# A level-embedding, attention and ternary-FFN tower on one core: load order, ScalarE's DMA queue, output copies and the written order of five engines changed

## The chip, the cores and the metric

One core of a Trainium2 chip runs the whole program once per launch. The metric is the device time of one execution in microseconds (us). Three runs of the kernel before gave 53.23, 53.73 and 56.08 us; their median, 53.73 us, is what the change is measured against.

## The reference, cut to what matters

Sixteen sequences of 128 token ids go in, a float32 array of shape [16, 128, 256] comes out.

```
level[b, s] = running count of open minus close brackets, clipped to 0..31        # a scan over s
h  = 0.15 * level_emb[level]                                                       # a table of 32 rows x 256
h  = h + attention(layernorm(h))      # 16 query heads of 16, 4 key/value heads; Wq, Wk, Wv, Wo, biases
W1t, W2t = ternary(W1), ternary(W2)   # clip(round(W / (mean|W| + eps)), -1, 1)
h  = h + relu(layernorm(h) @ W1t.T + b1) @ W2t.T + b2                              # 256 -> 1024 -> 256
```

A row of h depends on its level and its sequence alone, so everything is computed per sequence and level (16 x 32 = 512 rows), and the last step copies each row to the tokens that have its level.

## The kernel before, in words

The 16 sequences are taken as four groups g of four (NG = 4, BG = 4); a group has 128 rows, four sequences of 32 levels. The feed-forward part (FFN) works on two halves of 256 rows, hidden features in eight chunks of 128. No loop is left to a scheduler: each engine has a list of calls written out by hand (from line 457 for GpSimd, 598 for ScalarE, 956 for VectorE, 1300 for TensorE, 345 for SyncE), runs it strictly in that order, and meets the others at semaphores only. A call that waits holds up all that stands behind it on its engine.

The stages, with the names that the steps use:

- **Loads.** SyncE issues the table, Wq, Wk, Wv, bv, bk, then W1 in two halves, W2 in two halves, Wo, the broadcast table and biases (lines 345 to 362). ScalarE's queue issues the tokens (one load that reads x three times, into 48 partitions) and bq. Each load has a semaphore.
- **Levels.** `open_tokens`, `token_drops`, `drops`, `level_scan`, `level_ends`, `end_codes`, `gone_levels`, `level_onehot`, `count_blocks`, `counts`, `counts_out`: the scan, its smallest and largest level, a one-hot matrix and the number of tokens at each level.
- **Table and scores.** `table_stats` to `norm_table` normalise 32 table rows, `table_t` transposes them, `keys` and `queries` project them. `key_blocks` (line 793) adds bk and waits for its load. `key_hi`, `key_lo`, `query_lo` split into high and low parts. `scores`, `scores_t(g)`, `prefix_max`, `prefix_t`, `prefix_out`, `maxima`, `max_hi`, `max_parts`, `less_max` give each score less its maximum.
- **Attention.** `exps(g)`, `counted_values(g)` on GpSimd, `context(g)`, `inverse_sums(g)`, `normalise(g)`, `context_t(g)`, `ctx_out(g)`, `out_proj(g)`, `add_table(g)`, then the second layer norm: `row_stats`, `row_moments`, `variance_eps`, `inverse_root` (GpSimd), `norm_rows`, `rows_t`, `x_hi`, `x_lo`.
- **Ternary weights.** `magnitudes(w, i)` sums |W| of one half (ScalarE, waits for that half's load), `abs_total(w)` adds over partitions, `threshold(w)` makes the threshold and, for W1, the inverse. W1 is rounded by ScalarE (`rounded(q)`, then `ternary(q)`), W2 by VectorE (`signs(i)`, then `ternary(0..3)`). `weights_t(u)` transposes an eighth of the two matrices on TensorE, `weights_out(u)` copies it out.
- **FFN.** `ffn1(h, j)` is four matmuls of half h and chunk j; `hidden(h, j)` applies relu and b1, `hidden_lo(h, j)` splits; `ffn2(j, g)` adds two matmuls into the accumulator of group g. `final(g)` adds the residual.
- **Output.** `spread(g)` multiplies one-hot and final rows, four matmuls to four PSUM banks. `result(g)`: ScalarE copies sequences 0 and 1 to SBUF, VectorE 2 and 3. Each pair of sequences is one store of 256 KB, eight in all, the first of group 3 on ScalarE's queue (`last_store`), the others on SyncE's.

TensorE also runs matmuls of zeros (`warm_up`, `keep_warm`) where it would stand idle early on.

Of the kernel before, what the change touches and what calls it, by code (L numbers as in the profile page):

```python
# [27 lines left out]
P = 128  # L28
# [8 lines left out]
def level_tower(nc, x, emb, Wq, bq, Wk, bk, Wv, bv, Wo, bo, W1, b1, W2, b2, out):  # L37
# [20 lines left out]
    with ctx:  # L58
# [285 lines left out]
        def _(sp):  # L344
            sp.dma_start(emb1[:], emb).then_inc(d_emb, 16)
            sp.dma_start(wq[:], Wq.rearrange("(c p) n -> p c n", p=P)).then_inc(d_wq, 16)
            sp.dma_start(wk1[:], Wk.rearrange("(c p) n -> p c n", p=P)).then_inc(d_wk, 16)
            sp.dma_start(wv[:], Wv.rearrange("(c p) n -> p c n", p=P)).then_inc(d_wv, 16)
            sp.dma_start(bvr[:], bv.unsqueeze(0)).then_inc(d_bv, 16)
            sp.dma_start(bkc[:], bk.unsqueeze(0).unsqueeze(2).to_broadcast([2, KVD, 1])).then_inc(d_bk, 16)  # L350
            for i in range(2):
                c = slice(i * FC // 2, (i + 1) * FC // 2)
                sp.dma_start(w1[:, c, :], w1_rows[:, c, :]).then_inc(d_w1[i], 16)
            for i in range(2):
                sp.dma_start(w2[:, i, :], w2_rows[:, i, :]).then_inc(d_w2[i], 16)
# [9 lines left out]
            for g in range(NG):  # L365
                b0 = g * BG
# [8 lines left out]
        def _(pool):  # L375
# [80 lines left out]

            sequence_index()
            rounding_terms()
            level_index()
            diagonal_index()  # L460
            partition_index()
            column_index()
            ones_f32()
            level_replicas()
            root_power()
            table_root()
            ones_bf16()
            clip_bounds()
            scan_resets()
            group_selectors()  # L470
            table_copies()
            counted_values(0)
# [15 lines left out]
        def _(act):  # L488
            act.dma_start(tok3[:], x.unsqueeze(0).to_broadcast([3, B, S])).then_inc(d_tok, 16)
            act.dma_start(bq2[:], bq.rearrange("(k a e d) -> a e k d", k=KV, a=2, e=2)).then_inc(d_bq, 16)  # L490

# [61 lines left out]
            def last_store():  # L553
                b0 = (NG - 1) * BG
                act.wait_ge(a_out, NG)
# [42 lines left out]
            key_weights()  # L598
            query_weights(0)
            rows_out()  # L600
            query_weights(1)
            table_load()
# [3 lines left out]
            prefix_out()  # L606
            magnitudes(0, 1)
            max_hi()
            magnitudes(1, 0)
            magnitudes(1, 1)  # L610
            exps(0)
            exps(1)
            exps(2)
            rounded(0)
            ctx_out(0)
            ctx_out(1)
            exps(3)
            rounded(1)
            ternary(0)
            ctx_out(2)  # L620
            ternary(1)
            weights_out(0)
            ctx_out(3)
            x_hi(0)
            weights_out(1)
            x_hi(1)
            weights_out(2)
# [6 lines left out]
            hidden(0, 3)  # L634
            hidden(0, 4)
            norm_rows(2)
            hidden(0, 5)
            norm_rows(3)
            weights_out(6)
            x_hi(2)  # L640
            x_hi(3)
            hidden(0, 6)
# [4 lines left out]
            hidden(1, 2)  # L647
            hidden(1, 3)
            hidden(1, 4)
            final_hi(0)  # L650
            hidden(1, 5)
            hidden(1, 6)
            result(0)
            final_hi(1)
# [7 lines left out]
        def _(dve):  # L662
# [71 lines left out]
            def open_tokens():  # L734
                dve.wait_ge(d_tok, 16)
# [213 lines left out]
            def result(g):  # L949
                for b in range(2, BG):  # L950
                    dve.wait_ge(p_out, g * BG + b + 1)
                    ins = V.tensor_copy(osb[:, g, b, :], out_banks(g)[b][:, 0:D])  # L952
# [473 lines left out]
```

## Time and profile before

| what | value |
|---|---|
| median of 3 runs | 53.73 us (53.23 to 56.08) |
| profiled execution, its own time | 54.04 us |
| its span, first to last instruction | 52.0 us |
| TensorE busy | 45.6 us (88%), 394 matmuls |
| VectorE busy | 38.0 us (73%) |
| ScalarE busy | 34.2 us (66%) |
| GpSimd busy | 15.7 us (30%) |
| bytes moved | 5.37 MB, 103 GB/s over the span |
| share of TensorE in the chain that ended last | 76% |

The span is what the trace shows of one execution; 2.04 us of the execution's time lie around it. Busy shares are averages over stages with different limits. A busy TensorE is not one at its peak, and the matmuls of zeros count as busy. The chain of waits is followed back from the last instruction: each piece was released by the one before it.

### The profile page before, as it was taken

Reading aid. Unit: us, or ns where it says so; the run is one execution under the profiler, and the core shown is the slowest. Engines: PE = TensorE matmul, PEld = TensorE weight load, DVE = VectorE, ACT = ScalarE, POOL = GpSimd, SP = SyncE. Lnnn points to the kernel's source line nnn. Section 1 sums busy time; section 2 is a strip of 40 time slices with the busy share of each in tenths; the row PEclk is TensorE's granted clock in tenths of the full one; section 3 lists DMA queues with packets and bytes.
Section 4 is the critical chain, followed back from the end, with each engine's and each line's share of the span. In section 5 each row is a group of like instructions: output and inputs, shape, how many; then the busy total and the mean of one; then the engine's idle time right before and its main releaser. Section 6 shows DMA issues by size and latency. Waiting matters only on the chain.

```text
span 52.0 us, 1206 instructions
## 1 busy us (share of the span) xinstructions
PE 45.6 (88%) x394; PEld 36.3 (70%) x394; DVE 38.0 (73%) x141; ACT 34.2 (66%) x77; POOL 15.7 (30%) x37
## 2 busy tenths in 40 slices
PE   0999999999999799999999999999999999993000
PEld 0336469894758688768679999989999798860000
DVE  3558994698985289999999996269858889659100
ACT  0083231380799997989988999999967793509000
POOL 5689952000005950009200579970000000000000
PEclk9999999999999999999999999999999999999997
DMA  0183919999753100000000000000000005555893
GB/s 0 36 234 77 44 63 350 410 432 368 198 124 98 47 7 0 0 0 0 0 0 13 0 0 0 0 6 0 0 0 0 0 13 200 203 208 195 295 385 127
DMA packets 4658, 5.37 MB, mean 103 GB/s; under 512 B 1117, under 2 KB 4141, under 8 KB 4653
## 3 DMA queue, kind: packets, MB, share of 16 engines
q1 hardware_dynamic: 4312, 5.02, 31.2%
q10 hardware_dynamic: 341, 0.29, 1.6%
q8 instruction: 3, 0.05, 0.4%
q14 instruction: 2, 0.02, 0.1%
HBM read 3.21 MB, written 2.10 MB: 102 GB/s over the span
## 4 chain that ended last, share of the span: by engine, by line
PE 76%; DVE 10%; POOL 3%; issue 1%; ACT 1%; DVEq 1%
PE pswt L1258 16%; PE psmisc L1273 15%; PE psg L1067 8%; PE psg L1063 5%; PE psg L1194 4%; POOL rs L445 3%; PE psg L1240 3%; DVE aw L952 2%; PE psg L1106 2%; PE psg L1153 2%; PE psg L1203 2%; PE psg L1154 2%; PE psg L1158 2%; DVE cn L892 2%; DVE hq L906 2%; DVE st L910 2%
## 5 line engine op out<-in xcount | busy, mean ns | idle before, releaser
L587 ACT ACTIVATE hr<-pswt,b1c 128x256 f32<-128x256 f32 x16 | 7.6, 484 | 1.2 <-PE pswt L1258 0.9
L1273 PE MATMUL psmisc<-w2T,hh 128*128 128x256 f32 x32 | 8.2, 285 | 0.0
L1273 PE MATMUL psmisc<-w2T,hl 128*128 128x256 f32 x32 | 8.1, 281 | 0.0
L937 DVE TENSOR_TENSOR hl<-hr,hh 128x256 fp32r<-128x256 f32 x16 | 6.7, 435 | 1.2 <-ACT hh L589 0.9
L1258 PE MATMUL pswt<-xhi,w1T 128*128 128x256 f32 x32 | 7.0, 299 | 0.0
L1258 PE MATMUL pswt<-xlo,w1T 128*128 128x256 f32 x32 | 6.4, 280 | 0.0
L1273 PEld LDWEIGHTS psmisc<-w2T,hh 128*128 128x128 f32 x32 | 6.0, 189 | 0.1
L1273 PEld LDWEIGHTS psmisc<-w2T,hl 128*128 128x128 f32 x32 | 6.0, 189 | 0.0
L445 POOL TENSOR_TENSOR rs<-ve,mhalf 128x1 f32<-128x1 f32 x4 | 2.7, 686 | 9.1 <-DVE ve L918 9.1
L440 POOL TENSOR_TENSOR voc<-vo,cpos 128x272 f32<-128x272 f32 x4 | 2.7, 714 | 8.1 <-DVE cpos L858 8.1
L1258 PEld LDWEIGHTS pswt<-xhi,w1T 128*128 128x128 f32 x32 | 4.9, 189 | 0.3
L1258 PEld LDWEIGHTS pswt<-xlo,w1T 128*128 128x128 f32 x32 | 4.9, 188 | 0.0
L1067 PE MATMUL psg<-warm 128*128 128x256 bf16 x24 | 4.7, 352 | 0.0
L528 ACT ACTIVATE aw<-w 128x1024 f32<-128x1024 f32 x4 | 4.2, 1055 | 0.0
L1194 PE MATMUL psg<-wo,cT 128*128 128x256 f32 x16 | 4.2, 394 | 0.0
L594 ACT ACTIVATE aw<-psg 128x256 f32<-128x256 f32 x6 | 2.0, 381 | 2.9 <-PE psg L1298 1.6
L1067 PEld LDWEIGHTS psg<-warm 128*128 128x128 bf16 x24 | 2.8, 126 | 1.5 <-issue 0.8
L1063 PE MATMUL psg<-warm 128*128 128x512 bf16 x6 | 2.7, 630 | 1.2 <-DVE tiny L666 1.2
L589 ACT ACTIVATE hh<-pswt,b1c 128x256 fp32r<-128x256 f32 x7 | 3.4, 482 | 0.0
L502 ACT ACT_TABLE_LOAD x1 | 1.3, 1283 | 2.8 <-issue 2.8
L1194 PEld LDWEIGHTS psg<-wo,cT 128*128 128x128 f32 x16 | 2.8, 190 | 0.3
L455 POOL TENSOR_TENSOR hb<-hq,b_bc 128x256 f32<-128x256 f32 x4 | 3.0, 782 | 0.0
(177 smaller groups left out, 108.4 us busy)
## 6 DMA issues: line engine op xcount, KB each, us to landing
w<-in_L_ffn_W_dram SPq DMA_DIRECT2D x4, 512.0 KB, 6.8
out_dram<-aw SPq DMA_DIRECT2D x7, 256.0 KB, 2.4
wq<-in_L_attn_Wq_dram SPq DMA_DIRECT2D x1, 256.0 KB, 3.5
wo<-in_L_attn_Wo_dram SPq DMA_DIRECT2D x4, 64.0 KB
out_dram<-aw ACTq DMA_DIRECT2D x1, 256.0 KB, 2.9
emb<-in_L_tok_level_emb_dram SPq DMA_DIRECT2D x1, 128.0 KB
bo_bc<-in_L_attn_bo_dram SPq DMA_DIRECT2D x1, 128.0 KB, 8.8
b_bc<-in_L_ffn_b_dram SPq DMA_DIRECT2D x1, 128.0 KB, 7.3
```

The costliest lines, as they stand in the source:

```text
L440: nc.gpsimd.tensor_tensor(voc[:, bs, :], vo[:].unsqueeze(1).to_broadcast([P, BG, VW]), cpos[:, bs].unsqueeze(2).to_broadcast([P, BG, VW]), ...
L445: nc.gpsimd.tensor_tensor(rs2[:, g:g + 1], ve2[:, g:g + 1], mhalf[:], ALU.pow).then_inc(g_rs2, 1)
L455: nc.gpsimd.tensor_tensor(hb[:, g, :], hq[:, g, :], b2_bc[:], ALU.add).then_inc(g_hb, 1)
L528: nc.scalar.activation(aw[:, w, i * 1024:(i + 1) * 1024], halves(w, i), ACT.Abs, accum_out=asum[:, 2 * w + i:2 * w + i + 1]).then_inc(a_ab ...
L587: nc.scalar.activation(hr[:, n % NHR, :], pswt[n % 2][:, 0:RH], ACT.Relu, bias=b1c[:, j:j + 1]).then_inc(a_hr, 1)
L589: nc.scalar.activation(hh[:, n, :], pswt[n % 2][:, 0:RH], ACT.Relu, bias=b1c[:, j:j + 1]).then_inc(a_hh, 1)
L937: V.tensor_tensor(hl[:, n, :], hr[:, n % NHR, :], hh[:, n, :].bitcast(F32), ALU.subtract).then_inc(v_hl, 1)
L1063: mm(bank[:, :], warm[:, 0:P], warm[:], start=True, stop=True)
L1067: mm(bank[:, 0:256], warm[:, 0:P], warm[:, 0:256], start=True, stop=True)
L1194: ins = mm(psg[g][:, 0:D], cT[:, g, e].rearrange("p b l -> p (b l)"), wo[:, e, :], start=(e == 0), stop=(e == H2 - 1))
L1258: ins = mm(pswt[n % 2][:, 0:RH], w1T[:, j, k, :], part[:, k, HALF * h:HALF * (h + 1), :].rearrange("p g n -> p (g n)"), start=(m == 0 and ...
L1273: ins = mm(psmisc[r][:, 0:D], part[:, n, r * P:(r + 1) * P], w2T[:, j, :], start=(j == 0 and m == 0), stop=(j == FC - 1 and m == 1))
```

## The change

The computation is the same. Four things differ.

- **Loads.** SyncE issues table, Wq, W1 (two), bv, W2 (two), and the rest as before. Wk, Wv and bk go to ScalarE's queue, and the tokens are three loads of 16 partitions in place of one.
- **Copies.** `result(g)` has ScalarE copy sequences 0 and 2, VectorE 1 and 3, with a semaphore step at each copy.
- **Stores.** A pair's store waits for one copy of each engine; the waits of `spread` and `last_store` follow.
- **Written orders.** All four compute engines get new lists.

```diff
@@ sync
             sp.dma_start(emb1[:], emb).then_inc(d_emb, 16)
             sp.dma_start(wq[:], Wq.rearrange("(c p) n -> p c n", p=P)).then_inc(d_wq, 16)
-            sp.dma_start(wk1[:], Wk.rearrange("(c p) n -> p c n", p=P)).then_inc(d_wk, 16)
-            sp.dma_start(wv[:], Wv.rearrange("(c p) n -> p c n", p=P)).then_inc(d_wv, 16)
-            sp.dma_start(bvr[:], bv.unsqueeze(0)).then_inc(d_bv, 16)
-            sp.dma_start(bkc[:], bk.unsqueeze(0).unsqueeze(2).to_broadcast([2, KVD, 1])).then_inc(d_bk, 16)
             for i in range(2):
                 c = slice(i * FC // 2, (i + 1) * FC // 2)
                 sp.dma_start(w1[:, c, :], w1_rows[:, c, :]).then_inc(d_w1[i], 16)
+            sp.dma_start(bvr[:], bv.unsqueeze(0)).then_inc(d_bv, 16)
             for i in range(2):
                 sp.dma_start(w2[:, i, :], w2_rows[:, i, :]).then_inc(d_w2[i], 16)
...
-                if g < NG - 1:
-                    sp.wait_ge(a_out, g + 1)
-                    sp.dma_start(out_t[:, b0:b0 + 2, :], osb[:, g, 0:2, :]).then_inc(d_out, 16)
-                sp.wait_ge(v_out, g + 1)
-                sp.dma_start(out_t[:, b0 + 2:b0 + 4, :], osb[:, g, 2:4, :]).then_inc(d_out, 16)
+                for e in range(2):
+                    if g == NG - 1 and e == 0:
+                        continue
+                    b0 = g * BG + 2 * e
+                    sp.wait_ge(a_out, 2 * g + e + 1)
+                    sp.wait_ge(v_out, 2 * g + e + 1)
+                    sp.dma_start(out_t[:, b0:b0 + 2, :], osb[:, g, 2 * e:2 * e + 2, :]).then_inc(d_out, 16)
@@ scalar
-            act.dma_start(tok3[:], x.unsqueeze(0).to_broadcast([3, B, S])).then_inc(d_tok, 16)
+            for i in range(3):
+                act.dma_start(tok3[B * i:B * i + B, :], x).then_inc(d_tok, 16)
+            act.dma_start(wk1[:], Wk.rearrange("(c p) n -> p c n", p=P)).then_inc(d_wk, 16)
+            act.dma_start(wv[:], Wv.rearrange("(c p) n -> p c n", p=P)).then_inc(d_wv, 16)
             act.dma_start(bq2[:], bq.rearrange("(k a e d) -> a e k d", k=KV, a=2, e=2)).then_inc(d_bq, 16)
+            act.dma_start(bkc[:], bk.unsqueeze(0).unsqueeze(2).to_broadcast([2, KVD, 1])).then_inc(d_bk, 16)
...
-                act.wait_ge(a_out, NG)
+                act.wait_ge(a_out, 2 * NG - 1)
+                act.wait_ge(v_out, 2 * NG - 1)
...
-                for b in range(2):
+                for b in range(0, BG, 2):
                     act.wait_ge(p_out, g * BG + b + 1)
-                    ins = nc.scalar.activation(osb[:, g, b, :], out_banks(g)[b][:, 0:D], ACT.Copy)
-                ins.then_inc(a_out, 1)
+                    nc.scalar.activation(osb[:, g, b, :], out_banks(g)[b][:, 0:D], ACT.Copy).then_inc(a_out, 1)
@@ vector: open_tokens waits for 48 in place of 16; result(g)
-                for b in range(2, BG):
+                for b in range(1, BG, 2):
...
@@ tensor: spread
-                    if 1 <= g < NG - 1 and b % 2 == 0:
-                        pe.wait_ge((a_out, v_out)[b // 2], g)
+                    if 1 <= g < NG - 1:
+                        pe.wait_ge((a_out, v_out)[b % 2], 2 * (g - 1) + b // 2 + 1)
```

The written orders after the change (the orders before stand in the code above), the calls in the order in which each engine runs them:

```
GpSimd   diagonal_index ones_f32 partition_index ones_bf16 sequence_index level_index root_power column_index clip_bounds table_root
         rounding_terms level_replicas group_selectors table_copies scan_resets, then as before
ScalarE  key_weights rows_out query_weights(0) query_weights(1) query_hi(0) query_hi(1) magnitudes(0,0) (0,1) (1,0) (1,1) prefix_out max_hi
         rounded(0) exps(0) (1) (2) ternary(0) ctx_out(0) exps(3) ctx_out(1) weights_out(0) rounded(1) ctx_out(2) ternary(1) weights_out(1)
         table_load weights_out(2) ctx_out(3) x_hi(0) x_hi(1) weights_out(3) (4) hidden(0,0) (0,1) weights_out(5) hidden(0,2) (0,3)
         norm_rows(2) (3) hidden(0,4) (0,5) x_hi(2) (3) weights_out(6) hidden(0,6) (0,7) weights_out(7) hidden(1,0) (1,1) (1,2) final_hi(0)
         hidden(1,3) (1,4) (1,5) final_hi(1) result(0) hidden(1,6) (1,7) result(1) (2) (3) last_store
VectorE  partition_parts identity_f32 table_stats table_moments bias_selectors table_eps key_masks value_masks open_tokens mask_selectors
         token_drops drop_selectors norm_table level_scan key_blocks level_ends end_selectors spread_selectors key_hi query_lo(0) key_lo
         query_lo(1) gone_levels values end_codes prefix_max(0) (1) end_columns low_rows identities top_onehot level_onehot(0) (1) signs(0)
         count_blocks threshold(0) max_parts counts_out signs(1) threshold(1) ternary(0) inverse_sums(0) normalise(0) inverse_sums(1)
         normalise(1) inverse_sums(2) ternary(1) normalise(2) table_bias ternary(2) add_table(0) (1) row_stats(0) (1) row_moments(0)
         variance_eps(0) row_moments(1) inverse_sums(3) variance_eps(1) normalise(3) norm_rows(0) add_table(2) norm_rows(1) ternary(3)
         x_lo(0) (1) add_table(3) ... hidden_lo(1,0) final(0) hidden_lo(1,1) final_lo(0) hidden_lo(1,2) (1,3) (1,4) final(1) result(0)
         final_lo(1) hidden_lo(1,5) (1,6) (1,7) result(1) final(2) final(3) result(2) result(3)
TensorE  warm_up(6) keep_warm(12) table_t keep_warm(1) drops keep_warm(6) keys query_bias queries keep_warm(6) values scores scores_t(0)
         levels_out scores_t(2) level_ends prefix_t scores_t(1) abs_total(0) maxima scores_t(3) counts less_max abs_total(1)
         context(0) (1) (2) context_t(0) weights_t(0) context_t(1) out_proj(0) (1) context_t(2) weights_t(1) context(3) out_proj(2)
         weights_t(2) context_t(3) weights_t(3) rows_t(0) rows_t(1) out_proj(3) weights_t(4) ffn1(0,0) ffn1(0,1) weights_t(5)
         ffn1(0,2) (0,3) ffn2(0,0) (0,1) ffn1(0,4) ffn2(1,0) ffn1(0,5) weights_t(6) (7) rows_t(2) (3) ffn2(2,0) (2,1) ffn1(0,6) (0,7)
         ffn2(3,1) (4,0) (3,0) ffn1(1,0) ffn2(4,1) ffn1(1,1) ... ffn2(0,3) ffn1(1,7) spread(1) eleven ffn2 of groups 2 and 3 spread(2) spread(3)
```

## Rows read from the trace of the kernel before

**Rows 1.** Chain that ended last, pieces in order: start us, us, what

```profile
8.83 1.01 PE psg L1106 x8
15.81 0.60 PE psg L1166 x16
27.29 0.71 PE psg L1240 x8
46.08 0.77 PE psg L1298 x8
```

**Rows 2.** Timeline of the DMA issues (SPq SyncE, ACTq ScalarE): start us, us

```profile
0.72 0.38 SPq L345 DMA_DIRECT2D emb<-in_L_tok_level_emb_dram  x1
0.73 1.33 ACTq L489 DMA_DIRECT2D tok<-in_x_dram  x1
...
1.62 0.72 SPq L347 DMA_DIRECT2D wk<-in_L_attn_Wk_dram  x1
...
2.09 0.68 ACTq L490 DMA_DIRECT2D bq<-in_L_attn_bq_dram  x1
...
3.54 0.63 SPq L350 DMA_DIRECT2D bkc<-in_L_attn_bk_dram  x1
...
4.21 0.95 SPq L353 DMA_DIRECT2D w<-in_L_ffn_W_dram  x2
```

**Rows 3.** Windows of 0.5 us: engines' busy time, granted clock, DMA share, GB/s

```profile
6.00:6.50 0.50, 0.50 (x4) 0.31 (x3) 0.50 (x4) 0.00 (x0) 0.50 (x1) 1.00 0.01 0
9.50:10.00 0.50, 0.50 (x7) 0.47 (x7) 0.23 (x1) 0.12 (x1) 0.00 (x0) 1.00 1.06 434
```

**Rows 4.** Timeline of ScalarE, 10 to 19 us: start us, us

```profile
10.36 1.06 ACT L528 ACTIVATE aw<-w 128x1024 f32<-128x1024 f32 x1
13.27 0.38 ACT L520 ACTIVATE pmT<-psmisc 128x256 f32<-128x256 f32 x1 [1.76 <-PE psmisc L1141]
...
16.83 1.56 ACT L565 ACTIVATE et<-psg 128x512 f32<-128x512 f32 x3
...
18.26 1.26 ACT L537 ACTIVATE aw<-w,magic,inv 128x1024 f32<-128x1024 f32 x1
```

**Rows 5.** Timeline of VectorE and GpSimd, 8 to 28 us: start us, us

```profile
8.57 0.35 DVE L797 SCALAR_TENSOR_TENSOR ktm<-psmisc,bkc,km 128x128 f32<-128x128 f32 x1 [0.76 <-PE psmisc L1093]
13.30 0.68 DVE L867 TENSOR_SCALAR sg<-w 128x1024 bf16<-128x1024 f32 x1
13.90 0.34 DVE L821 TENSOR_SCALAR_CACHE_REDUCE oh<-pswt,pnum 128x128 fp32r<-128x128 f32 x1
14.99 0.34 DVE L863 SCALAR_TENSOR_TENSOR ms<-mhi,lowrow,psmisc 128x128 fp32r<-128x128 f32 x1
...
18.30 0.26 DVE L887 RECIPROCAL rec<-psg 128x16 f32<-128x16 f32 x1 [0.72 <-PE psg L1178]
23.49 1.49 POOL L445 TENSOR_TENSOR rs<-ve,mhalf 128x1 f32<-128x1 f32 x2 [4.57 <-DVE ve L918]
...
25.34 1.41 DVE L882 SCALAR_TENSOR_TENSOR tern<-aw,thr,sg 128x512 bf16<-128x512 f32 x2
...
26.67 0.74 DVE L926 TENSOR_TENSOR xlo<-psg,xhi 128x256 fp32r<-128x256 f32 x2
```

**Rows 6.** Chain that ended last, inside the FFN: start us, us, what

```profile
28.99 0.31 PE psg L1240 x4
...
37.91 0.47 PE pswt L1258 x4
...
39.79 0.71 PE psmisc L1273 x6
```

**Rows 7.** Timeline and windows of the end: start us, us; window, engines, DMA share, GB/s

```profile
46.74 0.66 ACT L594 ACTIVATE aw<-psg 128x256 f32<-128x256 f32 x2 [1.61 <-PE psg L1298]
...
47.43 0.37 SPq L369 DMA_DIRECT2D out_dram<-aw  x1
...
50.00:50.50 0.50, 0.00 (x0) 0.00 (x0) 0.00 (x0) 0.00 (x0) 0.00 (x0) 1.00 1.10 385
```

More of the change, by code:

```diff
@@ L605, in _ @@
             magnitudes(0, 0)
-            prefix_out()
             magnitudes(0, 1)
-            max_hi()
             magnitudes(1, 0)
             magnitudes(1, 1)
+            prefix_out()
+            max_hi()
+            rounded(0)
             exps(0)
@@ L613, in _ @@
             exps(2)
-            rounded(0)
+            ternary(0)
             ctx_out(0)
+            exps(3)
             ctx_out(1)
-            exps(3)
+            weights_out(0)
             rounded(1)
-            ternary(0)
             ctx_out(2)
             ternary(1)
-            weights_out(0)
+            weights_out(1)
+            table_load()
+            weights_out(2)
             ctx_out(3)
             x_hi(0)
-            weights_out(1)
             x_hi(1)
-            weights_out(2)
             weights_out(3)
@@ L634, in _ @@
             hidden(0, 3)
+            norm_rows(2)
+            norm_rows(3)
             hidden(0, 4)
-            norm_rows(2)
             hidden(0, 5)
-            norm_rows(3)
-            weights_out(6)
             x_hi(2)
             x_hi(3)
+            weights_out(6)
             hidden(0, 6)
@@ L999, in _ @@
             inverse_sums(2)
+            ternary(1)
             normalise(2)
             table_bias()
-            threshold(1)
-            ternary(0)
+            ternary(2)
             add_table(0)
+            add_table(1)
             row_stats(0)
-            add_table(1)
+            row_stats(1)
             row_moments(0)
-            row_stats(1)
-            inverse_sums(3)
             variance_eps(0)
             row_moments(1)
+            inverse_sums(3)
+            variance_eps(1)
             normalise(3)
-            variance_eps(1)
-            ternary(1)
             norm_rows(0)
+            add_table(2)
             norm_rows(1)
-            ternary(2)
             ternary(3)
@@ L1020, in _ @@
             x_lo(1)
-            add_table(2)
             add_table(3)
@@ L1301, in _ @@
             warm_up(6, psg[0])
-            keep_warm(8, psg[0])
+            keep_warm(12, psg[0])
+            table_t()
+            keep_warm(1, psg[0])
             drops()
-            keep_warm(5, psg[0])
-            table_t()
             keep_warm(6, psg[0])
@@ L1314, in _ @@
             levels_out()
+            scores_t(2)
             level_ends()
@@ L1361, in _ @@
             rows_t(3)
+            ffn2(2, 0)
+            ffn2(2, 1)
+            ffn1(0, 6)
             ffn1(0, 7)
-            ffn2(2, 1)
+            ffn2(3, 1)
+            ffn2(4, 0)
             ffn2(3, 0)
+            ffn1(1, 0)
             ffn2(4, 1)
-            ffn1(1, 0)
-            ffn2(4, 0)
             ffn1(1, 1)
```

146 lines of the change are left out of this document (70 added, 76 removed).

## The prediction

> **What bounds the kernel now.** I read the chain of waits first, then the timeline by stage. In the chain TensorE's pieces follow each other from the queries [rows 1] to 17.4 us, and again from 27.3 to 46.85 us. Between these lies the attention, where ScalarE, VectorE and GpSimd hand rows to each other. So there are four stages: up to `less_max` (ends 16.41 us, [rows 1]), attention and second norm (to the last `weights_t` before the FFN, end 28.00), the FFN (to 46.08), and the output. The matmuls of zeros early on are 6 + 8 + 5 + 6 + 5 ahead of `values` and after the change 6 + 12 + 1 + 6 + 6, one more.
>
> Why ScalarE matters: it sums |W1| of the first half at 10.36 us, then stands idle until `prefix_out` at 13.27, and the other three halves come behind it [rows 4]. The exponentials start at 16.83 and `rounded(0)` at 18.26. A half of W costs ScalarE about 1.04 us per start.
>
> The loads: nothing was moved at 6.0 to 6.5 us although W1 was issued at 4.21, behind bk (3.54); at 9.5 us they flow at 434 GB/s [rows 2, 3]. Two halves of W1 and two of W2, 2.1 MB, take about 5 us at that rate. In the output stage the stores run at 385 GB/s, all 16 engines busy [rows 7].
>
> **The loads, step by step.** W1 is issued behind Wq, near 1.6 us in place of 4.21, W2 from about 3.2. The halves land near 7 to 10 us. The use does not move: `magnitudes(0, 0)` stays behind `query_hi`, which waits for the queries (end 9.84, [rows 1]), so it starts at 10.36 as now. What the early weights permit is four halves in a row: 10.36 + 4 x 1.04 = 14.52 us.
> ScalarE's queue now issues tokens three times (0.38 us each, as the table's), Wk 0.72, Wv at most the same, bq 0.68, bk 0.63 [rows 2]: bk goes out at about 0.73 + 1.14 + 1.44 + 0.68 = 4.0 us and ScalarE is free at 4.6. Its table load of 1.28 us and the copy of Wk then end near 6.3 us; `rows_out` is needed near 6.8. Cost nothing; the cover is the zeros that TensorE runs until about 8.05 us. If it went, each further us on Wk would cost one.
> The tokens need about 3.7 us, as `drops` now stands later than `table_t`; also covered. `keys` starts at 8.05 to 8.1 as now, `scores` 0.1 us later by one more matmul of zeros.
> bk is the doubtful load. Key rows wait for it at 8.57 us [rows 5]; its own path (issue at 4.0 in place of 3.54, landed some time before 8.57) would bring it at the latest at 9.0, and VectorE has 0.6 us in hand there, since `key_lo` is now behind fewer calls. I take 0. Below: no gain can come from it. Above: it is a row of its own below.
>
> **Up to the first exponential.** `prefix_out` moves from 13.27 to 14.55, `maxima` (0.49 us) to 15.0, `max_hi` ends at 15.8. VectorE does four one-hots (0.28 us from start to start) from 14.1, then signs (0.68) before `threshold(0)`: the inverse is there at 16.35, and `max_parts` (0.34) ends at 16.65 in place of 15.33 [rows 5]. `less_max` (0.60, [rows 1]) then ends at 17.3: **0.9 us later**. On ScalarE `rounded(0)` runs from 16.4, and gives way at 17.55: exponentials **0.7 us later** than 16.83 [rows 4]. In return `rounded(0)` no longer stands between exponentials and `ctx_out(0)`, and VectorE does one of its four W2 pieces before the attention.
>
> **Attention and second norm.** The first `inverse_sums` moves from 18.30 to 19.0. From there to the end of the last `x_lo` of the half VectorE needs 9.1 us now (18.30 to 27.41). After the change it has one W2 piece less (0.70, half of the 1.41), no `threshold(1)` (0.2), and `add_table(2)` more (0.37) [rows 5]. Walking the list by starts: `add_table(0)` at 22.55 (two W2 pieces stand before it), `variance_eps(0)` 24.35, GpSimd's two roots (1.49) to 25.9, `norm_rows(1)` to 26.4, the last W2 piece to 27.1, `x_lo(1)` to 27.77. TensorE's `rows_t`, `out_proj(3)` and `weights_t(4)` fit before that; ScalarE's W1 pieces are out by 27.75, with about 0.5 us less in hand than the walk can err. So `ffn1(0, 0)` starts at 27.8, where it starts today (its piece of the chain follows 28.00, drain counted). Change 0, bounds -0.5 (roots and norms overlap better) and +0.7 (nothing is recovered of the delay).
>
> **FFN.** The work is the same, but `weights_t(5)` now lies behind the start: +0.27 (between 0.22 and the 0.31 of [rows 6]). Its ideal length: sixteen `ffn1` of 0.47, thirty-two `ffn2` of 0.235 (0.71 for three), two `weights_t`, rows and two spreads, 17.1 us; the chain takes 18.08 from 28.00 to 46.08 [rows 1, 6]. So 1.0 us is bubbles, at places where PE waited for ScalarE or changed stage. My walk of the new order finds about 0.5: `ffn2(4, 0)` waits 0.2 for `weights_out(6)`, and the rest is spread; the last eleven `ffn2` run without a gap, as now. Sum of the FFN: +0.27 - 0.5 = **-0.2** (-0.7 if no bubble is left, +0.3 if all stay).
>
> **Output.** ScalarE copied both sequences of a pair, 0.66 us from 46.74, and the store went out at 47.43 [rows 7]. With one copy on each engine the pair is in SBUF about 0.2 us earlier. The four last stores (1.05 MB at 385 GB/s, 2.7 us) are a block without gaps, so the end follows the first of them: **-0.2** (0 if the store engine is not ready, -0.33, half of ScalarE's two copies, at most).
>
> **Sum.** 0.0 (attention) - 0.2 (FFN) - 0.2 (output) = -0.4 us against the profiled execution's 54.04, hence 53.65. That execution is 0.31 above the median of 53.73, so I forecast 53.35, say **53.4 us**, under 1% faster. With all lower bounds: 53.73 - 0.5 - 0.7 - 0.33 = 52.2; with all upper ones 53.73 + 0.7 + 0.3 = 54.7.
>
> **Rivals.**
> 1. *bk lands late* (slower). bk is a load of single numbers: at 6.0 to 6.5 us, with W1 issued 1.8 us before and bk still in flight, no bytes to speak of moved [rows 2, 3]. So either such loads hold big ones up, or they suffer with them. After the change bk runs beside 2 MB of W. It decides from 9.1 us on, by which time `key_blocks` has used up its slack; from there one us late is one us on scores and all behind it. If bk waits until W has flowed (5 us at 434 GB/s from about 4.5, to 9.5, plus its own 2 us), it is 2.4 us late: 53.4 + 2.4 = **55.8 us**. Against it: at 6.0 it was W1 that stood still and not bk, and then only W is late, which has until 12.4 us. Chance 0.14.
> The Trainium skill, "DMA: Bandwidth & Descriptors", section "Issuing engines are not separate DMA queues", says that a second issuing engine saves only the time of issuing, as all loads share the same 16 engines. By that rule moving the small loads off SyncE's queue buys no bandwidth for them and they interleave with W; by it alone this rival's time would hold in full. No row here shows a small load of one queue beside a large one of the other (bk and W1 share one queue today).
> 2. *The delay before the attention is not recovered* (within 2%): the 0.7 us stays, FFN as forecast: 53.4 + 0.7 = **54.1 us**. For it: VectorE is packed from 19.0 to 27.8 in my walk, each slip counts. Together with all bubbles staying: 54.7. Chance 0.22, a quarter of it above 54.8.
> 3. *A faster middle* (faster): the new order hands rows without the waits of 0.2 to 0.3 us that now lie between ScalarE, VectorE and TensorE; FFN starts 0.5 earlier and has no bubble: **52.3 us**. Against it: the exponentials start later by sums of durations that hardly vary. Chance 0.2.
> 4. *Nothing moves* (the early weights are not used early, since `magnitudes` waits for queries, and the stores end as now): **53.7 us**. Chance 0.1.
> My forecast has 0.34.
>
> **Numbers.** The range 52.3 to 55.2 leaves out the far half of rival 1 and the tails of 2 and 3, about 2 in 10. Two per cent is 1.07 us, about what measuring this kernel can tell from no change: faster means below 52.66, slower above 54.80. Faster: rival 3 and a little of the forecast, 0.22. Slower: rival 1 and a part of 2, 0.2. Within: 0.58.
>
> **What would show it.** In the profile after: no idle ScalarE between four |W| halves from 10.4 to 14.5 us; exponentials from about 17.5; `rounded(0)` before them; `add_table(0)` near 22.5; `ffn1(0, 0)` at 27.8; last `ffn2` near 45.9; stores of group 2 and 3 without a gap from 0.8 us after the first issue. bk late shows as VectorE waiting at `key_blocks` for a load, and scores after 11.8. I am wrong if the exponentials start at 16.9 or before (then the plan gains 0.7 us that I don't give it), or if a second table load appears before them, as `table_load` now stands behind: the one load today precedes a copy and serves the exponentials too, so I cost it at nothing; a second would add its 1.28 us.

## The result, and the profile after

The changed kernel takes **62.52 us** (median of four runs, 61.81 to 67.68) against 53.68 (53.23 to 56.08): 1.156 times the time before, 95% interval 1.145 to 1.167. I had forecast 53.4, range 52.3 to 55.2. The profiled execution took 63.05 us, its span is 61.0. Every run of it shows a reduced TensorE clock in part of its span (mean 0.89 in the profiled one); runs of one kernel differ by how long that part is, so ratios and their intervals, here and below, are taken from the runs of each kernel that it lengthens least, and for some kernels the range says more than the median.

The chain of waits of the changed kernel (start us, us, what), with the pieces that answer to [rows 1, 6]:

```profile
3.13 9.21 DMA bq<-in_L_attn_bq_dram
12.34 0.14 issue
12.48 0.66 PE psg L1100 x2
13.13 1.85 PE psg L1107 x8
...
16.87 1.04 PE pswt L1125 x4
17.92 0.21 PE psmisc L1136
...
25.92 2.60 POOL voc L438 x3
...
36.59 0.25 PE psg L1241 x4
36.84 1.10 PE pswt L1259 x8
...
55.25 0.72 PE psg L1299 x8
```

In place of TensorE's zeros, a load now stands at the head of the chain: bq, issued at 3.13, holds the queries until 12.34. They start at 13.13 and take 1.85 us; before they started at 8.83 and took 1.01. The values (line 1125) end at 17.92, and the scores (line 1136) begin there. VectorE had the scores' last input ready 0.4 us sooner, and that path begins at bk:

```profile
15.21 0.35 DVE L799 SCALAR_TENSOR_TENSOR ktm<-psmisc,bkc,km 128x128 f32<-128x128 f32 x1 [7.30 <-DMA bkc<-in_L_attn_bk_dram]
...
17.26 0.23 DVE L815 TENSOR_TENSOR qs<-psg,qs 64x64 fp32r<-64x64 f32 x1
```

So two late loads hold the scores almost alike: bq through TensorE, bk through VectorE. The next list is the waits by engine and line (us in total, times, longest), the third the loads (KB each, us from issue to landing):

```profile
DVE ktm L799 <- DMA bkc<-in_L_attn_bk_dram: 7.3, 1, 7.3
...
ACT wk L504 <- DMA wk<-in_L_attn_Wk_dram: 4.4, 1, 4.4
```

```profile
wk<-in_L_attn_Wk_dram ACTq DMA_DIRECT2D x1, 64.0 KB, 8.5
wv<-in_L_attn_Wv_dram ACTq DMA_DIRECT2D x1, 64.0 KB, 9.6
```

Before the change the same rows read 3.2 us for Wk and 2.9 for Wv. So Wk comes at 10.6 us, and bk so late that `key_blocks` stands at 15.2 instead of 8.57 [rows 5]. The windows (engines' busy time, granted clock, DMA share, GB/s; answering to [rows 3]):

```profile
6.00:8.00 2.00, 1.96 (x13) 0.95 (x10) 1.01 (x3) 0.26 (x1) 0.80 (x1) 1.00 0.91 289
8.00:10.00 2.00, 0.00 (x0) 0.00 (x0) 0.00 (x0) 0.00 (x0) 0.00 (x0) 1.00 1.02 394
10.00:12.00 2.00, 0.80 (x4) 0.80 (x4) 0.00 (x0) 1.14 (x4) 0.73 (x4) 0.50 0.56 196
```

(The order in a row is PE, PEld, DVE, ACT, POOL.) From 8 to 10 us all five stand still while the loads, mostly W, flow at 394 GB/s. From 10 us the granted clock is 0.50 (1.2 GHz), until about 23.7. ScalarE's timeline, answering to [rows 4], and the end, to [rows 7]:

```profile
15.50 1.06 ACT L530 ACTIVATE aw<-w 128x1024 f32<-128x1024 f32 x1
...
18.63 1.04 ACT L530 ACTIVATE aw<-w 128x1024 f32<-128x1024 f32 x1
...
26.41 1.08 ACT L568 ACTIVATE et<-psg 128x512 f32<-128x512 f32 x2
```

```profile
56.46 1.43 SPq L369 DMA_DIRECT2D out_dram<-aw  x3
57.13 0.40 ACTq L559 DMA_DIRECT2D out_dram<-aw  x1
```

The four |W| halves stand in a row as planned, but from 15.5. The account of the 9.0 us between the two profiled executions, stage by stage:

| stretch | before | after | difference |
|---|---|---|---|
| to the first exponential | 16.83 | 26.41 | +9.58 |
| from it to `ffn1(0, 0)` | 11.17 | 10.43 | -0.74 |
| from there to `spread(2)` | 18.08 | 18.41 | +0.33 |
| `spread(2)` to the end of the span | 5.92 | 5.75 | -0.17 |

The cuts are those of the prediction; `ffn1(0, 0)` is this piece of the chain before, and the one at 36.84 after:

```profile
28.00 1.00 PE pswt L1258 x8
```

All that was lost was lost ahead of the attention. The attention is 0.7 us shorter, which the prediction had; the FFN is 0.3 longer, where it had -0.2.

One thing about the column "before". In its profiled execution TensorE's early zeros still took 0.24 us each at 6 us, in that of a kernel with the same orders and loads (copies_only, below) 0.13:

```profile
5.93 1.18 PE psg L1067 x5
```

```profile
5.79 0.65 PE psg L1067 x5
```

(First the kernel before, then copies_only.) The granted clock reads 1.00 in both. The first exponential of copies_only stands at 16.16 and not at 16.83, so the 16.83 that the prediction walked from holds about 0.7 us of a slow start that is not in the same stretch of copies_only.

### The profile page after: what moved, and what is told of

Same layout as the page of the kernel before. It is cut to its first block, busy times and chain, and to the rows that moved or that the text cites. A ratio compares the mean times of both kernels' runs of the same rounds, so it can differ in the third digit from the quotient of the medians.

```text
span 61.0 us, 1212 instructions
## 1 busy us (share of the span) xinstructions
PE 51.0 (84%) x392; PEld 40.0 (66%) x392; DVE 38.5 (63%) x141; ACT 34.2 (56%) x77; POOL 15.8 (26%) x37
## 4 chain that ended last, share of the span: by engine, by line
PE 60%; DMA 15%; DVE 7%; POOL 4%; ACTq 4%; issue 1%; DVEq 1%; ACT 0%; POOLq 0%
DMA bq<-in_L_attn_bq_dram 15%; PE psmisc L1274 13%; PE pswt L1259 13%; PE psg L1195 5%; POOL voc L438 4%; PE psg L1107 3%; PE psg L1154 3%; ACTq L488 2%; PE psg L1155 2%; PE psg L1068 2%; PE psg L1159 2%; PE psg L1241 2%; DVE aw L954 2%; PE pswt L1125 2%; PE psg L1204 1%
## 5 line engine op out<-in xcount | busy, mean ns | idle before, releaser
L438 POOL TENSOR_TENSOR voc<-vo,cpos 128x272 f32<-128x272 f32 x4 | 3.2, 824 | 13.9 <-DVE cpos L860 13.9
L1068 PE MATMUL psg<-warm 128*128 128x256 bf16 x25 | 5.3, 379 | 0.0
L1068 PEld LDWEIGHTS psg<-warm 128*128 128x128 bf16 x25 | 3.4, 141 | 1.6 <-issue 0.6
L1094 PE MATMUL psmisc<-xT,wk 128*128 128x32 f32 x4 | 1.1, 406 | 3.2 <-ACT xT L512 3.2
```

The source lines that it names most:

```text
L438: nc.gpsimd.tensor_tensor(voc[:, bs, :], vo[:].unsqueeze(1).to_broadcast([P, BG, VW]), cpos[:, bs].unsqueeze(2).to_broadcast([P, BG, VW]), ...
L1068: mm(bank[:, 0:256], warm[:, 0:P], warm[:, 0:256], start=True, stop=True)
```

## Experiments

Theory A: the small loads on ScalarE's queue land late beside W, and TensorE's fallen clock adds to it. Rivals: the new orders cost the time; the clock alone does. The kernel before took 53.3 to 53.6 us beside them.

**plan_only**: orders, copies and stores of the change, loads of before.

```diff
+            sp.dma_start(wk1[:], ...); sp.dma_start(wv[:], ...); sp.dma_start(bvr[:], ...); sp.dma_start(bkc[:], ...)   # ahead of W1
-            act.dma_start(wk1[:], ...); act.dma_start(wv[:], ...); act.dma_start(bkc[:], ...)                            # tokens in one load
```

> The changed kernel with the loads of the kernel before (small loads ahead of W on SyncE's queue, tokens in one load); written orders, copies and stores stay changed. Theory A (the small loads starve behind W on ScalarE's queue, and that is all of the loss): ScalarE's copy of Wk starts near 5 us in place of 10.6, bk is there when the keys are, TensorE's clock stays full from 7 us; time 53.0 to 54.6 us. Rival B (the new orders cost as well, since the magnitudes stand ahead of the maxima): 56 us or more.

54.26 us (54.24 to 54.28), ratio 1.014 (1.009 to 1.019). The chain starts at W and goes through the last |W| halves and the maxima:

```profile
5.65 8.04 DMA w<-in_L_ffn_W_dram
13.72 1.15 ACT aw L529 x2
14.89 0.39 ACT pmT L521
...
27.79 0.25 PE psg L1240 x4
...
46.47 0.72 PE psg L1298 x8
```

```profile
L567 ACT ACTIVATE et<-psg x4: 592/595/605, 17.6 to 21.1; 128x512 f32<-128x512 f32 x4
```

(Durations ns, first and last start.) So the orders cost about 0.7 us, not 9. The exponentials start at 17.6: 0.8 later than in the profiled kernel before, 1.4 later than in copies_only.

**loads_only**: the kernel before with the changed loads alone (the reverse edit).

> The kernel before with the changed loads alone (W behind Wq, Wk, Wv and bk on ScalarE's queue, tokens in three loads); all written orders, copies and stores as before. Theory A: the copy of Wk starts near 10.5 us and bk lands near 15; time 61 to 63 us. Rival B: the orders carry a good part of the 8.8 us, so this stays under 59 us.

63.18 us (62.4 to 64.3); in the profiled run (62.40):

```profile
L798 DVE SCALAR_TENSOR_TENSOR ktm<-psmisc,bkc,km x1: 350/350/350, 14.7 to 14.7; 128x128 f32<-128x128 f32 x1
its engine sat idle before it (us, times) until:
  DMA bkc<-in_L_attn_bk_dram: 5.6, 1
```

The loads alone are the loss. They are not so at a full clock: the granted clock reads 1.00 in every window of 6 to 30 us, but until about 23 us TensorE's matmuls took the time that they take at a half clock elsewhere. The same matmul here and in hot_wait (below):

```profile
17.66 0.53 PE psg L1154
```

```profile
17.65 0.28 PE psg L1154
```

In every other kernel here the durations and the granted clock agree from 7 us on. What the loads cost at a full clock is therefore read from hot_wait, not from this run.

**wk_sync**: the changed kernel with Wk back on SyncE's queue ahead of W1.

```diff
             sp.dma_start(wq[:], ...)
+            sp.dma_start(wk1[:], ...)
-            act.dma_start(wk1[:], ...)
```

> The changed kernel with Wk alone moved back to SyncE's queue, between Wq and W1. Theory A1 (each small load behind it is late for the same reason, so the next one takes over): Wk is copied near 6.5 us, keys at 8.1, then the queries wait for bq until some 11 us and key_blocks for bk until 13 to 14; time 58 to 61 us. Rival A2 (Wk's 256 packets are what fills ScalarE's queue; without them bq and bk come at once): queries end before 10.5, bk by 9.5; time under 55.5 us.

64.21 us (62.68 to 66.16), ratio 1.175, longer than the 58 to 61 that I expected. Wk is copied at 5.79 and bq has come by 9.1, but bk lands no sooner, and `key_blocks` stands at 15.0:

```profile
3.92 10.95 DMA bkc<-in_L_attn_bk_dram
```

**w_held**: SyncE waits for bk before it issues W. **w_held_bv**: the same, bv also ahead of the wait.

```diff
             sp.dma_start(wq[:], ...)
+            sp.dma_start(bvr[:], ...)        # w_held_bv alone
+            sp.wait_ge(d_bk, 16)
```

> The changed kernel with one added wait: SyncE issues W1 and all behind it only when bk has landed; the small loads stay on ScalarE's queue in the changed order. Theory A (they are late because W moves beside them): Wk copied by 6.5 us, bk landed by 8.7, W1's first half near 11.5, so the magnitudes start 1 us late and the halves of W2 bound them: 54 to 56.5 us. Rival C (ScalarE's queue is slow by itself, or its issues are): bk lands after 12 us even with W held, and the time is over 60 us.

60.74 us (58.72 to 62.05). With W out of the way Wk is copied at 6.27 and bk is there at 7.24, all on the same queue as in the change; `key_blocks` at 8.57 waits for no load. But bv, now behind W1, is late (12.3 us), and W itself: the |W| halves start at 11.3 to 15.5, each about when its load is in. The time missed the 54 to 56.5 that I expected, and rival C's reason, a bk later than 12 us, did not hold either.

> As w_held (W1 and all behind it issued once bk has landed), but bv issued ahead of the wait, so that it is not behind 1 MB of W1. In w_held the keys came at 8.1 us and bk at 8.5, and TensorE then stood from 10.2 to 12.3 for bv and lost its clock at 13.9. Theory A (small loads beside W is the whole fault): values at 10.3 us, scores by 11.6, clock full throughout, magnitudes from 11.3 bound by W's landing to about 16.6; time 55.0 to 56.5 us. Rival C (holding back W costs as much as it gives): 58 us or more.

58.03 us (55.97 to 59.15). The median is what rival C had; the 55.97, the one run with a granted clock of 0.996, is inside the theory's range. In the profiled run (57.95) the clock is half from 17.9 to 24.7 us. The chain has bk's landing with nothing of W beside it, and then W's:

```profile
4.39 2.82 DMA bkc<-in_L_attn_bk_dram
...
8.57 6.88 DMA w<-in_L_ffn_W_dram
...
16.64 0.39 ACT pmT L523
```

So bk needs 2.8 us when W is held back. Holding W back trades one wait for another.

**w_512**: the changed kernel, W1 and W2 as eight loads in 512-byte packets instead of four in 4096-byte ones; the bytes and their place are the same.

```diff
+                for h in range(2):
+                    cols = slice(h * P, (h + 1) * P)
+                    sp.dma_start(w1[:, c, cols], w1_rows[:, c, cols]).then_inc(d_w1[i], 16)   # W2 alike
```

> The changed kernel with each half of W loaded as two loads of half its columns, so that every packet of W is 512 bytes in place of 4096; same bytes, same queue, same order. Theory D (on a DMA engine the two queues take turns packet by packet, so a small packet waits for one big one each time, 159 ns for 4096 bytes, 26 ns for 512): Wk is copied at 6.3 to 7 us, bk (64 packets on each of two engines) lands by 10.5, time 55 to 58 us. Rival E (the small loads wait for W's bytes, however they are cut): Wk copied after 9.5 us, bk after 14, time over 61 us.

The loads (KB each, us to landing) and the key rows:

```profile
wk<-in_L_attn_Wk_dram ACTq DMA_DIRECT2D x1, 64.0 KB, 4.7
wv<-in_L_attn_Wv_dram ACTq DMA_DIRECT2D x1, 64.0 KB, 5.3
```

```profile
L803 DVE SCALAR_TENSOR_TENSOR ktm<-psmisc,bkc,km x1: 351/351/351, 10.5 to 10.5; 128x128 f32<-128x128 f32 x1
```

Wk lands in 4.7 us instead of 8.5, `key_blocks` stands at 10.5 instead of 15.2. One execution would not be enough for Wk, since its landing varies: in the six profiled kernels here in which it is issued on ScalarE's queue beside W in large packets it takes 5.8 to 8.5 us. But w_512_hot has 4.7 again, and `key_blocks` at 10.5 in both stands against 14.3 to 15.2 in the five with large packets in which bk is issued behind Wk or Wv. So the small loads lose by the size of W's packets, not by its bytes. The time was 62.05 (55.31 to 63.67), the clock half from 11.7 to 28.8 us in the profiled run; the run of 55.31 had 0.98.

**hot_wait**: the changed kernel with 30 more matmuls of zeros ahead of the keys and 20 behind the queries. **w_512_hot**: w_512 with 18 and 14 more.

```diff
-            keep_warm(6, psg[0])      # ahead of keys(); behind queries() alike
+            keep_warm(36, psg[0])     # 26 behind queries(); w_512_hot: 24 and 20
```

> The changed kernel with 30 more matmuls of zeros ahead of the keys and 20 more ahead of the values, so that TensorE is never idle while it waits for Wk, bq and bk. Theory F (a part of the loss is TensorE at 1.2 GHz from 10.0 to 23.7 us, which the idle time from 7.9 to 11.2 brought on): clock full throughout, scores at about the same 17.6 us, less_max 1.5 to 2.5 us sooner after the scores; time 59 to 60.5 us. Rival G (the clock costs nothing, since the engines around it bound the stage): 61.8 us or more.

60.07 us (59.82 to 62.4), ratio 1.121 (1.112 to 1.131), granted clock 1.00 in every window of 2 to 34 us.

```profile
L568 ACT ACTIVATE et<-psg x4: 575/588/596, 23.6 to 26.9; 128x512 f32<-128x512 f32 x4
```

`key_blocks` stands at 14.3, the exponentials 9.3 us behind it; in the changed kernel they are 11.2 behind. The scores start here:

```profile
17.43 0.12 PE psmisc L1136
```

From the scores to the exponentials it is 6.20 us, and 6.20 to 6.22 in the three other kernels with added zeros; in the changed kernel 8.49 (17.92 to 26.41). So the half clock costs 2.3 us in this stretch alone. My zeros cost something too: they end at 16.48 and the values behind them at 17.43, while VectorE was done at 16.6. Without them the scores could have started 0.7 us earlier.

> The changed kernel with W1 and W2 in 512-byte packets (eight loads), and 18 and 14 more of the zeros matmuls in the two gaps of TensorE in which its granted clock fell (before the keys, and behind the queries). Theory (packet turns cost the landings, the clock the rest): landings as with 512-byte packets before (Wk copied near 6.9, bk near 10.5, scores near 13), clock full from 5.3 on in every run, and 56 to 57.5 us: 54.3 for the new orders plus 2 to 3 of the 2.4 us that the scores are later than in the kernel that has only the orders. Rival (the clock was not what made that kernel slow, its longer W issues or its late W did): 60 us or more with a full clock.

57.38 us (57.29 to 57.85), ratio 1.079 (1.067 to 1.090). `key_blocks` at 10.5, exponentials at 20.9, of which 1.7 us is my own zeros: they end at 13.7 and the scores start at 14.66, where in w_512 they start at 12.94. That it is 2.7 us faster than hot_wait doesn't measure the landings, since my zeros end 2.8 us sooner here (13.71 against 16.48). The better sign of the gain is w_512's one run at a clock of 0.98, 55.31 us; it is a single run and was not profiled.

**copies_only**: the kernel before with the changed copies and stores.

> The kernel before with the changed copies and stores alone (sequences 0 and 2 copied by ScalarE, 1 and 3 by VectorE, stores by pairs of one copy each). Prediction's term: the first store of group 2 is issued 0.2 us earlier behind its first matmul and the block of four last stores moves with it: minus 0.2 us, ratio 0.996. Rival: no change, since the stores' 2.85 us block is bound by when VectorE is through.

53.34 against 53.50 us, ratio 0.997 (0.994 to 1.001): the term of -0.2 is neither shown nor excluded; the last row of the table above (-0.17) agrees with it.

**row_after, row_before, row_plan**: bk as one row of two 256-byte pieces, added by a matmul with ones, in the changed kernel, in copies_only and in plan_only.

```diff
-            act.dma_start(bkc[:], bk.unsqueeze(0).unsqueeze(2).to_broadcast([2, KVD, 1]))
+            act.dma_start(bkr[:], bk.unsqueeze(0).unsqueeze(0).to_broadcast([1, 2, KVD]))
+                mm(psmisc[1][:, 0:L], bkr[:].rearrange("o r n -> o (r n)"), ones[0:1, 0:L], start=True, stop=False)
```

> The changed kernel, but bk arrives as one row of two 256-byte pieces (same place, last of ScalarE's loads) and is added to the keys by one more matmul with a row of ones, in place of 128 pieces of 4 bytes and an add per partition. Theory (the landings of the small loads are counted in packets, so 128 four-byte ones cost as much time beside W's 4096-byte ones as 128 big ones): Wk still copied near 10.6 us and bq still waited for till near 12.3, but the key blocks then wait on no DMA and stand at about 12.5 instead of 15.2, scores near 15 instead of 17.7; time 59 to 60.5 against 62.5 (the 2.7 us, less the extra matmul). Rival (the delay is one of bytes queued or of bq's and Wv's place, bk's pieces were only last in line): the row lands as late as the pieces did, near 15, and now holds TensorE as well: 62 to 63. If the granted clock still falls between 7.9 and 11 us, about 2 us of the excess stays in either case.

The row lands at 10.08 and `key_blocks` stands at 11.3; the chain names the row's landing, and Wk's copy ends at the same time (10.10). The time is 66.35 us (61.57 to 66.7), above the 59 to 60.5 that I expected: three of the four runs have a mean clock of 0.80 to 0.84. The profiled one is the fourth, at 0.91; its clock is half from 11.6 to 21.9 us and its exponentials start at 24.6.

```profile
4.38 5.70 DMA bkr<-in_L_attn_bk_dram
```

> The kernel before with the change's copies and stores, and with bk as one row of two 256-byte pieces (in bk's old place ahead of W1 on SyncE's queue), added by a matmul with ones. In the kernel before bk's 128 four-byte pieces ran from 4.9 to 7.4 us while W1's first packets took 2.1 us each. Theory: W's four halves land 1.5 to 2 us earlier (last near 11.7), the key blocks stay at 8.6 or 0.1 earlier (they were behind the keys, not behind bk), and the first exponential moves at most 0.3 us, since the magnitudes were not what ended the wait there: 53.0 to 53.4 against 53.3 for the copies alone. Rival: W's rows were the hidden bound of the attention's start: 52.5 or less. Second rival: the extra matmul and PE's wait for the row delay the keys: 53.8.

55.38 us (54.03 to 58.63), ratio 1.014 (1.003 to 1.025) from its two runs near 54.1. W's last packet is in at 12.1 us instead of 13.2, but the exponentials start at 16.7, where copies_only, its own base, has them at 16.16. The queries come 0.54 us later (8.70 against 8.16), behind the added matmul and its wait for the row. That was my second rival, which had 53.8 us. 

> The changed kernel's orders, copies and stores with the loads of before, and bk as one row of two 256-byte pieces ahead of W1. Its counterpart without the row took 54.3 us, and its chain of waits began with W's last half (5.65 to 13.7 us) and went through the last magnitudes, the maxima and the rounding. Theory: the last half lands near 11.7, so the magnitudes (four in a row in that order) end 1 to 1.5 us earlier, the scales 1 us earlier, and the time is 53.2 to 53.7: level with the kernel before or a little under. Rival: the scores and the context bound it as soon as W is earlier by 0.3 us, and it is the order of the exponentials behind the magnitudes and the rounding that costs: 54.0 to 54.3, nothing gained.

56.69 us (54.23 to 62.65), ratio 1.018 (1.006 to 1.030): nothing gained over plan_only. Its profiled run was one of 62.65, and shows what neither the theory nor the rival allowed for; windows as above:

```profile
8.00:9.00 1.00, 1.00 (x9) 0.85 (x8) 0.18 (x1) 0.00 (x0) 0.00 (x0) 1.00 1.07 389
9.00:9.50 0.50, 0.50 (x6) 0.50 (x5) 0.50 (x4) 0.00 (x0) 0.00 (x0) 1.00 0.93 336
9.50:10.00 0.50, 0.50 (x6) 0.50 (x6) 0.50 (x3) 0.00 (x0) 0.00 (x0) 0.60 1.00 401
10.00:10.50 0.50, 0.50 (x4) 0.44 (x5) 0.21 (x2) 0.07 (x1) 0.00 (x0) 0.50 1.02 418
```

TensorE was busy in each of them and its clock fell all the same.

Open after these twelve was which load costs what.

**bk_moved**: plan_only with bk alone moved to ScalarE's queue, behind bq.

```diff
-            sp.dma_start(bkc[:], ...)      # ahead of W1
             act.dma_start(bq2[:], ...)
+            act.dma_start(bkc[:], ...)
```

> The changed kernel's orders, copies and stores with the loads of before, and one load moved: bk, from SyncE's queue ahead of W1 to ScalarE's queue behind bq. So its 128 four-byte pieces run beside W's 4096-byte packets, but with nothing of Wk and Wv ahead of them on their queue. Its counterpart with bk ahead of W1 took 54.3 us. Theory (what delayed bk was the queue ahead of it, 512 pieces of Wk and Wv and then bq): bk lands by 7 to 8.5 us, the key blocks stand at 8.2 to 9, and the time is 54.0 to 54.9. Rival (the four-byte pieces themselves starve beside W's packets): key blocks at 10.5 or later, 56.5 us or more.

59.52 us (57.62 to 61.85; its clock 0.94 to 0.85). bk lands 6.8 us after its issue, and `key_blocks` waits:

```profile
2.78 6.82 DMA bkc<-in_L_attn_bk_dram
```

```profile
9.72 0.35 DVE L798 SCALAR_TENSOR_TENSOR ktm<-psmisc,bkc,km 128x128 f32<-128x128 f32 x1 [2.61 <-DMA bkc<-in_L_attn_bk_dram]
```

Between my two cases: 1.6 us later than in plan_only (8.15), more than the queue ahead explains, since of these loads only the tokens and bq are ahead of it there. The exponentials are 3.4 us later (20.96), and the clock is half from 11.5 to 18.3 us, so a part of that is the clock. The windows of 5 to 6 us, with bk on either queue (here, then plan_only):

```profile
5.00:6.00 1.00, 0.98 (x9) 0.62 (x7) 0.62 (x1) 0.08 (x1) 1.00 (x1) 1.00 1.04 37
```

```profile
5.00:6.00 1.00, 1.00 (x8) 0.67 (x7) 0.70 (x2) 0.00 (x0) 1.00 (x1) 1.00 1.85 58
```

37 and 58 GB/s: W almost stands still while bk's pieces run, whichever queue they are on.

**row_after_hot**: row_after with 30 and 6 more zeros matmuls.

> The changed kernel with bk as one row at the end of ScalarE's loads, and 30 and 6 more of the zeros matmuls in TensorE's two gaps, so that its granted clock has no reason to fall. With the row alone the key blocks stood at 11.3 us instead of 15.2, but the clock was half from 12 to 24 us and the time 61.6. Theory (in every kernel so far the end came 36.4 to 37.2 us behind the first exponential, and the exponential 9.3 to 9.5 us behind the key blocks where the clock was full): key blocks at 11.3, first exponential near 21, 57.4 us (56.9 to 58.3), with the clock above 0.97 in every run; against the 60.0 of the kernel with the zeros and bk's 128 pieces, bk's pieces were worth 2.5 us. Rival (bk's pieces hid another bound, the maxima, W's magnitudes or the counts): first exponential near 23.5 and 59.5 to 60.

58.84 us (58.59 to 59.42), ratio 1.100 (1.093 to 1.108), full clock. My zeros held the keys up (they end at 11.95), so `key_blocks` stood at 12.9, the exponentials at 22.7. It is 1.2 us faster than hot_wait, but this says nothing of bk's pieces: in both kernels the scores start behind my second zeros, and hot_wait has 14 more of those. They end at 16.48 there and at 15.52 here, 0.96 us apart, and so are the exponentials (23.63 and 22.67). What bk's pieces are worth at a full clock is not shown, nor are the 2.5 us that I expected.

**wv_last_hot**: hot_wait with Wv's load behind bq and bk.

```diff
             act.dma_start(bq2[:], ...); act.dma_start(bkc[:], ...)
+            act.dma_start(wv[:], ...)      # was ahead of bq
```

> The changed kernel with 30 and 20 more zeros matmuls, and Wv's load put behind bq and bk on ScalarE's queue instead of ahead of them. With Wv in its place the kernel with these zeros took 60.0 us, its key blocks at 14.3. Theory (each load waits for every packet ahead of it on its queue, and each of Wv's 16 per DMA engine takes a turn with one of W's big ones): bq and bk land some 2 to 2.5 us earlier, key blocks near 12, 57.8 to 58.3 us, Wv itself landing at 12 to 13, before the values that come behind the scores' inputs; if values wait for Wv, half a us more. Rival (W's bytes set when the small loads come, whatever their order): key blocks stay at 14 or later and the time at 60.

60.93 us (59.57 to 61.98), ratio 1.121 (1.110 to 1.131): the rival held. Wk lands in 6.5 us instead of 7.5, which is within what it varies by, and bk not earlier:

```profile
L799 DVE SCALAR_TENSOR_TENSOR ktm<-psmisc,bkc,km x1: 351/351/351, 14.5 to 14.5; 128x128 f32<-128x128 f32 x1
```

So "each load waits for the pieces ahead of it" is too simple for bk; why it took until 14.4 here I can't say.

## Why the prediction was wrong

**The step that failed** is the pricing of the small loads on ScalarE's queue. For bk it reads "would bring it at the latest at 9.0" and "I take 0"; for Wk, "Cost nothing", with "the copy of Wk then ends near 6.3 us"; bq has no landing time at all. I priced these loads by their issue (bk out at 4.0; it was 4.40) and took their flight time from a kernel in which nothing large ran beside them. With W in flight bk holds `key_blocks` until 15.21, 6.2 us behind my latest time; bq holds TensorE until 12.34; Wk needs 8.5 us instead of 3.2 and is copied from 10.6. With W held back, the same loads on the same queue are in time: Wk is copied from 6.27 (until 6.69), bk is there at 7.24.

Of the three, Wk was not the one that counted: wk_sync had it copied at 5.79 and bq in by 9.1, and `key_blocks` still stood at 15.0 behind bk. The condition "if it went, each further us on Wk would cost one" did come up and had neither a chance nor a place in the range; no run shows what Wk alone costs.

**bk.** Rival 1 named the right load and the right place, at 0.14, and mis-sized it: 2.4 us late, because bk was to have the engines to itself once W had flowed by 9.5. W flowed to 11.5, and bk needed 3.5 us more, with Wo and the broadcast loads beside it. Its argument against itself ("it was W1 that stood still and not bk") was read off a stretch in which bk had no competitor ahead of it: bk_moved shows that W all but stands still and bk is late as well (6.8 us against 2.8 with W held back). Nor had `key_blocks` the slack that I gave it: in plan_only and copies_only it already waits for bk, 0.8 and 0.5 us.

The Trainium skill, "DMA: Bandwidth & Descriptors", section "Issuing engines are not separate DMA queues", which I had weighed, held: a second issuing engine saved only issue time, and the loads interleaved with W. In this trace 445 of Wk's and Wv's 512 pieces start between 6.5 and 9.0 us, and 169 of W's 4096-byte packets start in the same stretch.

The Trainium skill, same page, section "Queues, rings and completion order", says that an engine goes round the queues that it has work for packet by packet, a packet being several pieces. w_512 fits such turns: with W's packets an eighth as large, Wk's landing fell to 4.7 us. It does not settle the price, since it has only a typical number of pieces for a packet and not that of these loads. An estimate after the fact, with one turn for each small piece: Wk and Wv are 512 pieces of 256 bytes, 32 for each of 16 engines; a 4096-byte packet of W takes 159 ns in the trace, so 32 turns are 5.1 us, and the pieces ran from 5.5 to 11.5. But 445 small ones beside 169 large are 2.6 for one, so one for one is not what happened while most of them ran, and that the sum comes near is luck.

**The clock** stood nowhere in the text. TensorE stood idle from 7.95 to 11.2 us, its granted clock was half from 10.0 to about 23.7, and the stretch from scores to exponentials took 8.49 us instead of the 6.20 of hot_wait.

An estimate of the shares of the 9.58 us in the first row of the table: at a full clock the changed kernel's exponentials would stand at 15.21 (`key_blocks`) + 2.42 (from there to the scores, as in w_512) + 6.20 (to the exponentials, as in hot_wait) = 23.83. That leaves 2.58 for the clock (to 26.41), 6.24 for the loads (from plan_only's 17.59) and 0.76 for the orders (from 16.83).

**Up to the first exponential.** The number was right, 0.7 later, at 17.5; plan_only has 17.6. The way to it was not, and this is luck. The prediction had W early and the four |W| halves from 10.36. In plan_only the queries, and with them the first half, come 0.5 us sooner, and W is as late as before: the maxima wait for its last half (lands 13.69). row_plan comes nearest to the plan: with W 1.1 us earlier than in plan_only, its two best runs (54.23 and 54.36) gain nothing; it has no profile at a full clock.

**Attention** (0, nothing left of the delay): right. From the first exponential to `ffn1(0, 0)` it is 11.17 us before, 10.45 in plan_only and 10.43 in the changed kernel, so the middle gives back the 0.7 us, and plan_only's `ffn1(0, 0)` stands at 28.04 against 28.00. Rival 2 had that delay stay. The time of plan_only, 54.26, is near its 54.1, but not for its reason.

**FFN** (-0.2, at most +0.3): wrong. It measured +0.33 in the changed kernel and +0.35 in plan_only (18.08 before and in copies_only, 18.41 and 18.43 after). I had +0.27 for `weights_t(5)` and -0.5 for bubbles that the new order would remove; no such gain shows. **Output** (-0.2) measured -0.17 in the span; copies_only can't resolve it from nothing. No second table load stands before the exponentials, as I costed it.

## What to carry to other kernels

A load's landing time holds only for what ran beside it. Before moving small loads to another queue so that a large one can start earlier, measure their landing with it in flight: here bk took 2.8 us with W held back, 6.8 beside W, and over 10 beside W and behind Wk and Wv. Then ask which of them the first matmuls and the steps behind them wait for, and leave those ahead of it. Where a wait can leave TensorE idle early on, price the granted clock as well: here 2.3 us on a stretch of 6.2. And look at what added zeros hold up: two of my comparisons measured where the zeros ended.

## What the runs showed of the hardware

- A load of 128 four-byte pieces all but stops a 4096-byte-packet load on its own queue and on another: 58 and 37 GB/s in the stretch of 5 to 6 us; the loads flow at 394 from 8 to 10 in the changed kernel.
- The end of the execution follows the first exponential by 36.4 to 37.3 us in the thirteen profiled kernels in which the clock is full, or full again, by then, so this one start tells their time. It is 37.9 to 39.0 where the half clock lasts beyond it (w_held, w_held_bv, w_512, row_plan).
- The granted clock can read 1.00 while matmuls take nearly twice their time: 0.53 us for one of 0.28, and so until about 23 us, in loads_only. The durations of one and the same matmul are the check.
- The granted clock fell behind TensorE's idle stretch in the changed kernel, but in row_plan also with TensorE busy throughout and DMA at 336 to 418 GB/s; plan_only, the same but for bk's form, kept a mean of 0.976 to 0.996 in four runs of four. What decides that is open, and no version here beats the kernel before by more than copies_only's unresolved 0.3%.
